# Two graph-attention blocks on one core: edge rows transposed on TensorE, wide one-hots, four reordered steps, and a weight chunk's low part moved to GpSimd

## The reference

```python
def gat_conv(x, src, dst, W, a_src, a_dst, b, heads, out_ch):
    h = (x @ W).reshape(n, heads, out_ch)
    alpha_src = jnp.einsum('nhc,hc->nh', h, a_src)
    alpha_dst = jnp.einsum('nhc,hc->nh', h, a_dst)
    e = jax.nn.leaky_relu(alpha_src[src] + alpha_dst[dst], 0.2)
    p = jnp.exp(e - segment_max(e, dst)[dst])
    alpha = p / segment_sum(p, dst)[dst]
    return segment_sum(h[src] * alpha[:, :, None], dst).reshape(n, heads * out_ch) + b
# block 0, self loops added to src and dst:
h = jax.nn.elu(gat_conv(x, src, dst, W1, a_src1, a_dst1, b1, 8, 768))
out = gat_conv(h, src, dst, W2, a_src2, a_dst2, b2, 1, 768)
```

## Time and profile before

| | |
|---|---|
| median of 3 runs | 361.6 us (361.49 to 362.41) |
| the profiled execution's own time | 363.34 us |
| span of its profile | 361.5 us |
| mean granted TensorE clock | 0.993 |
| TensorE (PE) busy | 349.8 us, 97% |
| VectorE (DVE) busy | 213.7 us, 59% |
| ScalarE (ACT) busy | 218.7 us, 60% |
| GpSimd (POOL) busy | 242.5 us, 67% |

### The profile page before, as it was taken

How to read it: one execution, slowest core, us unless ns; L and a number is a source line. 1 busy time by engine, 2 the same in 40 slices (tenths; PEclk the granted TensorE clock), 3 DMA queues, 4 the chain that set the end, 5 groups by cost and what they waited for, 6 DMA issues and landing times.

```text
span 361.5 us, 6079 instructions
## 1 busy us (share of the span) xinstructions
PE 349.8 (97%) x2058; PEld 300.3 (83%) x2060; DVE 213.7 (59%) x545; ACT 218.7 (60%) x376; POOL 242.5 (67%) x163
## 2 busy tenths in 40 slices
PE   7999999899999999999999999999999999999994
PEld 3888888788988988998898898888767888788883
DVE  4999872436418235553641834455687797953776
ACT  5897595637754864673775486467276867264601
POOL 2389659483883967669397496856256898687911
PEclk9999999899999999999999999999999999999999
DMA  7888967356556546574654665567162657337002
GB/s 248 284 301 227 397 229 258 130 176 173 175 163 198 166 170 188 169 244 130 222 178 136 214 172 174 188 167 245 57 199 94 181 190 196 131 113 233 5 2 87
DMA packets 24544, 65.15 MB, mean 180 GB/s; under 512 B 1952, under 2 KB 3024, under 8 KB 24528
## 3 DMA queue, kind: packets, MB, share of 16 engines
q1 hardware_dynamic: 20864, 55.02, 45.7%
q10 hardware_dynamic: 3664, 9.92, 10.0%
HBM read 64.15 MB, written 0.79 MB: 180 GB/s over the span
## 4 chain that ended last, share of the span: by engine, by line
PE 79%; DMA 4%; DVE 4%; POOL 4%; issue 4%; ACT 3%; DVEq 0%; POOLq 0%; SPq 0%
PE ps L1006 56%; PE ps L1296 9%; PE ps L1094 6%; POOL ring_lo L370 3%; DMA raw<-in_L_gnn_W 3%; PE ps L1128 2%; PE ps L1360 2%; DMA b_rows<-in_L_gnn_b 1%; PE ps L1073 1%; ACT ring_hi L357 1%; PE ps L1058 1%; DVE stats L1740 1%; DVE ps L1960 1%; POOL x_sb L634 1%; DVE z L1967 1%
## 5 line engine op out<-in xcount | busy, mean ns | idle before, releaser
L370 POOL TENSOR_TENSOR ring_lo<-raw,ring_hi 128x768 fp32r<-128x768 f32 x92 | 167.1, 1850 | 75.6 <-ACT ring_hi L357 75.6
L357 ACT ACTIVATE ring_hi<-raw 128x768 fp32r<-128x768 f32 x96 | 77.4, 839 | 40.0 <-PE ps L1006 28.9
L386 POOL TENSOR_TENSOR ring_lo<-raw,ring_hi 128x512 fp32r<-128x512 f32 (+1 forms) x40 | 59.4, 1512 | 20.3 <-ACT ring_hi L379 20.2
L1006 PE MATMUL ps<-ring_hi,zT_hi 128*128 128x256 f32 (+1 forms) x256 | 69.3, 346 | 0.9 <-ACT zT_hi L808 0.9
L1006 PE MATMUL ps<-ring_lo,zT_hi 128*128 128x256 f32 (+1 forms) x256 | 67.1, 337 | 0.0
L1006 PE MATMUL ps<-ring_hi,zT_lo 128*128 128x256 f32 (+1 forms) x256 | 66.8, 338 | 0.0
L1513 DVE CUSTOM_DVE_ANT_0 e<-ps,att 128x768 f32<-128x768 f32 x38 | 34.2, 953 | 49.0 <-PE ps L1006 49.0
L1006 PE MATMUL ps<-ring_hi,xT_hi 128*128 128x512 f32 x192 | 52.0, 347 | 2.1 <-DVE zT_lo L1662 1.8
L1006 PE MATMUL ps<-ring_hi,xT_lo 128*128 128x512 f32 x192 | 50.5, 341 | 0.0
L1006 PE MATMUL ps<-ring_lo,xT_hi 128*128 128x512 f32 x192 | 50.5, 339 | 0.0
L1006 PEld LDWEIGHTS ps<-ring_hi,zT_hi 128*128 128x128 f32 x256 | 42.0, 189 | 7.1 <-ACT zT_hi L808 1.6
(11 more groups left out here) (172 smaller groups left out, 545.1 us busy)
## 6 DMA issues: line engine op xcount, KB each, us to landing
raw<-in_L_gnn_W SPq DMA_DIRECT2D x54, 768.0 KB, 4.4
raw<-in_L_gnn_Wr SPq DMA_DIRECT2D x8, 768.0 KB, 4.5
att<-in_L_gnn_a_src ACTq DMA_DIRECT2D x10, 384.0 KB, 3.7
att<-in_L_gnn_a_dst ACTq DMA_DIRECT2D x10, 384.0 KB, 4.9
raw<-in_L_gnn_W SPq DMA_DIRECT2D x4, 384.0 KB, 5.1
x_sb<-in_x SPq DMA_DIRECT2D x3, 256.0 KB, 4.9
rows_hc<-in_L_gnn_b SPq DMA_DIRECT2D x1, 512.0 KB, 7.8
rows_hc<-in_L_gnn_g SPq DMA_DIRECT2D x1, 512.0 KB, 8.6
```

What stands on the lines that cost most here:

```text
L357: eng.activation(slot_hi(c), raw_chunk(c), ACT.Copy).then_inc(hi_done, 1)
L370: eng.tensor_tensor(slot_lo(c), raw_chunk(c), slot_hi(c).bitcast(F32), ALU.subtract)\
L386: eng.tensor_tensor(ring_lo[:, q["ring_at"]:q["ring_at"] + w], raw[:, q["raw_group"], q["raw_at"]:q["raw_at"] + w], ring_hi[:, q["ring_at" ...
L1006: last = pe.matmul(ps[:, at + to:at + to + hi - lo], a, b[:, lo:hi], start=start and n == 0 and to != D, stop=stop and n == PASSES - 1, sk ...
```

## The change

Seven edits, all in block 0's first two heads and the opening:

1. Head 1 on ScalarE: the DMAs of head 2's attention rows go behind the six splits of phase 3, just ahead of `elu(1)`. In the loop the order stays as it was.
2. Head 0 on VectorE: the fourth attention dot of head 1 goes from ahead of `elu(0)` to behind its first piece.
3. Edge lists: loaded as 64 rows of 128 edges, cast, transposed on TensorE in chunk 0, copied from PSUM. The edges of a tile are thus other ones; their sum is the same.
4. Input: x's first two chunks get separate high parts; chunks 0 and 2 begin with the pass that needs only high parts; the third part of x uses the first one's place in PSUM, behind a wait. The warm-up is cut, the bias rows' DMA goes ahead of the first split and their transpose from chunk 1 to chunk 2.
5. Steps 20 to 31 carry the weight (two per-partition scalars each; steps 26 to 31 count from below with negative weight).
6. One-hots 20 to 31 are made without a weight, by two wide operations.
7. FIRST = 3: GpSimd makes chunk 3's low part, and the second load of phase 1 waits for it.

The diff, cut to its core (declarations of tiles and semaphores are left out):

```diff
DVE_CH = CH - POOL_CH
-FIRST = 4
+FIRST = 3
 PHASES = 2 * H0
...
 AM_AT = [T_AT, S_AT + N]
-XT_AT = 0
+XT_AT = [0, BANK, 2 * BANK, 2 * BANK + N, 0, N]
 B1_AT = T_AT
+EDGES_AT = S_AT + N + 2 * ET
 STEPS_AT = T_AT + N - 1
...
 STEPS_EARLY = 5
+BELOW_FROM = (ACT_STEPS + ET) // 2
+PLAIN = ((ACT_STEPS, 24), (24, ET))
 PACK = 4096.0
...
-            if isinstance(p, int) and p == 1 and 2 * (g + 1) <= FIRST:
-                sp.wait_ge(lo_by["dve"], 2 * (g + 1))
-            else:
+            if isinstance(p, int) and p == 1 and 2 * g < FIRST:
+                sp.wait_ge(lo_by["dve"], min(2 * (g + 1), FIRST))
+            if not (isinstance(p, int) and p == 1 and 2 * (g + 1) <= FIRST):
                 sp.wait_ge(lo_by["pool"], POOL_CH * p - POOL_CH + 2 * (g + 1) - FIRST)
...
     load_x(0)
-    sp.dma_start(edges[:, 0, :], src.rearrange("(p t) -> p t", p=P)).then_inc(edges_loaded, 16)
-    sp.dma_start(edges[:, 1, :], dst.rearrange("(p t) -> p t", p=P)).then_inc(edges_loaded, 16)
+    sp.dma_start(edge_rows[0:ET, :], src.rearrange("(t p) -> t p", p=P)).then_inc(edges_loaded, 16)
+    sp.dma_start(edge_rows[ET:2 * ET, :], dst.rearrange("(t p) -> t p", p=P)).then_inc(edges_loaded, 16)
     sp.dma_start(raw[:, 0, D:2 * D], w1[:, 1, 0, :]).then_inc(raw_full[0], 16)
...
     pool.wait_ge(b2_loaded, 16)
-    pool.wait_ge(xT_ps, 3)
+    pool.wait_ge(xT_ps, 4)
     for i in range(NT):
...
     act.activation(rstd[:, 0:1], half[:, :], ACT.Exp)
+    act.dma_start(b1_rows[:, :], b0_b1.rearrange("(t p) -> t p", p=P)).then_inc(b1_loaded, 16)
...
-    def input_hi(b):
-        act.wait_ge(xT_ps, b + 1)
-        act.activation(xT_hi[:, 2 * b:2 * b + 2, :].rearrange("p k n -> p (k n)"),
-                       ps[:, XT_AT + b * BANK:XT_AT + (b + 1) * BANK], ACT.Copy).then_inc(xT_hi_done, 1)
+    def input_hi(first, chunks, at_done):
+        act.wait_ge(xT_ps, at_done)
+        act.activation(xT_hi[:, first:first + chunks, :].rearrange("p k n -> p (k n)"),
+                       ps[:, XT_AT[first]:XT_AT[first] + chunks * N], ACT.Copy).then_inc(xT_hi_done, 1)
     split_hi(act, FIRST_PHASE, 0, reused=False)
-    act.dma_start(b1_rows[:, :], b0_b1.rearrange("(t p) -> t p", p=P)).then_inc(b1_loaded, 16)
-    input_hi(0)
+    input_hi(0, 1, 1)
+    input_hi(1, 1, 2)
     split_hi(act, FIRST_PHASE, 1, reused=False)
...
     split_hi(act, FIRST_PHASE, 2, reused=False)
-    input_hi(1)
+    input_hi(2, 2, 3)
     steps(3, 5)
     split_hi(act, FIRST_PHASE, 3, reused=False)
-    input_hi(2)
+    input_hi(4, 2, 4)
     load_att(0, b0_as1[0:1, :], b0_ad1[0:1, :], D, reused=False)
...
         exps(h, (1, 0))
-        after_exps(h, last)
-    def after_exps(h, last=False):
         att_for(h + 1, last)
+        after_exps(h)
+        elu(h)
+    def after_exps(h):
         for c in range(4):
...
             split_hi(act, 2 * h + 1, c)
-        elu(h)
...
     after_exps(1)
+    att_for(2)
+    elu(1)
     with act.Fori(2, H0 - 1) as h:
...
-    def keep_warm(times, at):
+    def keep_warm(times, at, width=BANK):
...
         for _ in range(times):
-            pe.matmul(ps[:, at:at + BANK], zeros[:, 0:P], zeros[:, :], start=True, stop=True)
+            pe.matmul(ps[:, at:at + width], zeros[:, 0:P], zeros[:, 0:width], start=True, stop=True)
...
     pe.wait_ge(zeros_set, 1)
-    keep_warm(8, PROJ)
+    keep_warm(7, PROJ)
+    keep_warm(2, PROJ, P)
...
         pe.wait_ge(x_loaded[b], 16)
+        if b == 2:
+            pe.wait_ge(xT_lo_done, 1)
         for k in (2 * b, 2 * b + 1):
             for i in range(NT):
-                at = XT_AT + k * N + i * P
+                at = XT_AT[k] + i * P
                 last = pe.transpose(ps[:, at:at + P], x_sb[:, i, k * P:(k + 1) * P], ident[:, :])
-        last.then_inc(xT_ps, 1)
+            if b == 0 or k % 2 == 1:
+                last.then_inc(xT_ps, 1)
     transpose_x(0)
-    keep_warm(2, PROJ + 2 * BANK)
     for c in range(CH):
-        if c == 1:
+        if c == 2:
             pe.wait_ge(b1_loaded, 16)
...
         if c in (0, 2):
-            pe.wait_ge(xT_hi_done, c // 2 + 1)
-            chunk(FIRST_PHASE, c)
-            for passes in (FIRST_TWO, LAST_ONE):
+            pe.wait_ge(xT_hi_done, c + 1)
+            pe.wait_ge(hi_done, c + 1)
+            for passes in ((0,), (1,), LAST_ONE):
+                if passes == (1,):
+                    chunk(FIRST_PHASE, c)
                 if passes is LAST_ONE:
                     pe.wait_ge(xT_lo_done, c // 2 + 1)
+                if passes is LAST_ONE and c == 0:
+                    pe.wait_ge(edges_cast, 1)
+                    pe.wait_ge(iota_cast, 2)
+                    pe.transpose(ps[:, EDGES_AT:EDGES_AT + 2 * ET], edge_rows_f[:, :],
+                                 ident[0:2 * ET, 0:2 * ET]).then_inc(edges_ps, 1)
                 for i in range(NT):
...
         for t in range(ET):
-            pe.wait_ge(hot_done, t + 1)
+            pe.wait_ge(hot_done, t + 1 if t < ACT_STEPS else ACT_STEPS + sum(first <= t for first, _ in PLAIN))
             if t < ACT_STEPS:
...
     def input_lo(b):
-        dve.wait_ge(xT_hi_done, b + 1)
-        dve.tensor_tensor(xT_lo[:, 2 * b:2 * b + 2, :].rearrange("p k n -> p (k n)"),
-                          ps[:, XT_AT + b * BANK:XT_AT + (b + 1) * BANK],
-                          xT_hi[:, 2 * b:2 * b + 2, :].rearrange("p k n -> p (k n)").bitcast(F32),
+        dve.wait_ge(xT_hi_done, b + 2)
+        at, apart = XT_AT[2 * b], XT_AT[2 * b + 1] - XT_AT[2 * b]
+        of = ps[:, at:at + 2 * apart].rearrange("p (k n) -> p k n", k=2)[:, :, 0:N]
+        dve.tensor_tensor(xT_lo[:, 2 * b:2 * b + 2, :], of, xT_hi[:, 2 * b:2 * b + 2, :].bitcast(F32),
                           ALU.subtract).then_inc(xT_lo_done, 1)
...
     dve.tensor_copy(iota_ps, iota_i).then_inc(iota_cast, 1)
+    def plain_hots(first, end):
+        at = (first % per_home) * 2 * N
+        home = hot_homes[first // per_home][:, at:at + (end - first) * 2 * N]
+        shape = [P, end - first, P]
+        dve.tensor_tensor(home.rearrange("p (t n) -> p t n", n=2 * N)[:, :, 0:P],
+                          iota_ps[:, 1:1 + P].rearrange("p (t n) -> p t n", t=1).to_broadcast(shape),
+                          row_of[:, first:end].rearrange("p (t n) -> p t n", n=1).to_broadcast(shape),
+                          ALU.is_equal).then_inc(hot_done, 1)
...
     split_lo(dve, FIRST_PHASE, 0)
+    dve.wait_ge(edges_loaded, 32)
+    dve.tensor_copy(edge_rows_f[:, :], edge_rows[:, :]).then_inc(edges_cast, 1)
     input_lo(0)
-    dve.wait_ge(edges_loaded, 32)
-    dve.tensor_copy(edges_f[:, :, :], edges[:, :, :]).then_inc(edges_cast, 1)
-    dve.wait_ge(edges_cast, 1)
+    dve.wait_ge(edges_ps, 1)
+    dve.tensor_copy(edges_f[:, :, :].rearrange("p s t -> p (s t)"), ps[:, EDGES_AT:EDGES_AT + 2 * ET])\
+       .then_inc(edges_placed, 1)
+    dve.wait_ge(edges_placed, 1)
     dve.tensor_scalar(src_bias[:, :], edges_f[:, 0, :], -1.0, 0.5, ALU.mult, ALU.add).then_inc(src_biased, 1)
...
     dve.tensor_tensor(row_of[:, :], edges_f[:, 1, :], upper[:, :], ALU.subtract).then_inc(edges_split, 1)
-    for at, end, scale in ((0, ACT_STEPS, 1.0), (ACT_STEPS, ET, 2.0)):
+    for at, end, scale in ((0, ACT_STEPS, 1.0), (ACT_STEPS, BELOW_FROM, 2.0), (BELOW_FROM, ET, -2.0)):
         dve.tensor_scalar(weight_of[:, at:end], upper[:, at:end], scale * (PACK + 1.0) / P, -scale,
...
         for t in range(first, end):
-            dve.tensor_scalar(step(t), iota[:, :], edges_f[:, 0, t:t + 1], -0.5, ALU.is_ge, ALU.add)\
-               .then_inc(step_dve_done, 1)
+            dve.tensor_scalar(step(t), iota[:, :], edges_f[:, 0, t:t + 1], weight_of[:, t:t + 1],
+                              ALU.is_lt if t >= BELOW_FROM else ALU.is_ge, ALU.mult).then_inc(step_dve_done, 1)
...
     dve.wait_ge(iota_cast, 2)
+    dve.wait_ge(edges_split, 5)
     late_steps(ACT_STEPS, ACT_STEPS + STEPS_EARLY)
...
     late_steps(ACT_STEPS + STEPS_EARLY, ET)
-    split_lo(dve, FIRST_PHASE, 3)
     input_lo(2)
...
        .then_inc(b1_ready, 1)
-    dve.wait_ge(edges_split, 4)
-    hots(0, ET)
+    hots(0, ACT_STEPS)
+    for first, end in PLAIN:
+        plain_hots(first, end)
...
-    def elu(h):
+    def elu(h, between=None):
         for q in range(3):
+            if q == 1 and between is not None:
+                between()
             if q >= 1:
...
     dots(1, a_s, 0, a_src_done)
-    dots(1, a_d, 1, a_dst_done)
-    elu(0)
+    dots(1, a_d, 1, a_dst_done, tiles=(0,))
+    elu(0, between=lambda: dots(1, a_d, 1, a_dst_done, tiles=(1,)))
     dve.wait_ge(z_lo_done, 3)
...
```

More of the change, by code:

```diff
@@ L139, in build_gnn @@
         iota = sb("iota", [P, 1 + N], BF16)
-        edges = sb("edges", [P, 2, ET], I32)
+        edge_rows = sb("edge_rows", [2 * ET, P], I32)
+        edge_rows_f = sb("edge_rows_f", [2 * ET, P])
         edges_f = sb("edges_f", [P, 2, ET])
@@ L244, in build_gnn @@
         edges_cast = sem("edges_cast")
+        edges_ps = sem("edges_ps")
+        edges_placed = sem("edges_placed")
```

## The result

The changed kernel takes 365.63 us (median of 6 runs, 364.8 to 367.84), the kernel before on the same chip 361.55 (6 runs, 361.37 to 363.55): ratio 1.0099, 95% interval 1.0072 to 1.0126. It is slower by 4.1 us by the medians and by 3.6 by the ratio, where 3.5 less had been forecast. Rival (b), the alternating hold, had given 365.7. The six times fall into two groups, 364.8 to 364.9 and 366.3 to 367.8; the profiled execution is of the lower one.

What follows compares the result with a forecast made beforehand. The prediction took TensorE, busy 97% of the span, as the bound; 3.6 + 0.65 + 0.6 - 1.4 = 3.5 us off the median 361.6 gave 358.1 us, range 356.0 to 361.8.

Steps and rivals of the forecast that it cites:

- Rival (b): Opening: GpSimd's low parts and VectorE's late steps alternate; 7.2 stall and 1.8 clock on 356.7 give 365.7; chance 0.22.
- Part (5): Opening, chunk 3's low part on GpSimd: one hold against VectorE's seven late steps, costing 1.4; bounds 0 and 7.2.
- Part (1): Passage to head 2: moving its attention-row DMAs makes head 2 a steady head, 3.6 off; bounds 0 and 3.64.
- Part (2): Head 0's elu: with the fourth dot behind its first piece, VectorE and TensorE start earlier, 0.65 off.
- Part (3): Opening: chunk 1 starts at 9.45, chunk 2 at 12.2 against 12.72; with chunk 4's wait, 0.6 off.
- Part (4): Steps and one-hots: seven late steps 1.9, two wide one-hots 1.9, sums wait for TensorE's edge count, not them; 0.
- the 0.16 that chunk 4 was said to wait: Opening: chunk 4's wait for GpSimd at 17.05 before the change, counted towards the opening's 0.6.

Runs made afterwards that it cites:

- experiment 1: The changed kernel with chunk 3's low part back on VectorE, all else kept: 360.01 us, ratio to the kernel before 0.9962.
- experiment 7: The changed kernel with chunk 3's low part back on VectorE and the full warm-up of before restored: 359.88 us, ratio to the kernel before 0.9945.
- Experiment 6: The kernel before, unchanged, run once more for its trace: 361.37 us.
- experiment 4: The kernel before with only chunk 3's low part moved to GpSimd, steps keeping one per-partition scalar: 362.04 us, ratio 1.0003.
- experiment 5: The kernel before with only the two reorderings of heads 0 and 1, run twice: 359.26 us and 359.1 us.
- experiment 9: The kernel before with the two reorderings and the bias rows' DMA early, their transpose at chunk 2, run twice: 359.11 us and 358.81 us.
- experiment 8: The kernel before with the two reorderings and the changed kernel's short warm-up: 359.95 us, ratio 0.9938.
- experiment 3: The changed kernel with the last part of xT_lo made ahead of the seven late steps: 365.32 us, ratio to the kernel before 1.012.
- experiment 2: The changed kernel with the seven late steps reading iota from PSUM instead of SBUF: 360.85 us, ratio to the kernel before 0.9959.

## Why the prediction was wrong

**Part (5), the low part on GpSimd, is the step that failed.** It charged "one hold", 1.4, out of bounds of 0 and 7.2. The mechanism was named rightly, one engine holds the other, and its size chosen wrongly: the hold is paid anew for every step that meets GpSimd at work. "Two steps may follow each other so closely that nothing gets between" was the argument against rival (b); the timeline shows that each GpSimd operation does get between. The part cost 5.0 (experiment 1). The rows give the same: chunk 4 starts at 21.27, and with the low part on VectorE at 17.87 (experiment 7's profile). That is 3.4, and the low clock adds 1.7. The 3.4 are less than the stall of 3.93 because in experiment 7's profile x's transposes begin 0.26 later (5.56 against 5.30) and TensorE waits 0.18 for chunk 3's low part.

Rival (b) named the right mechanism, with 7.2 of stall and 1.8 of clock. Its stall was too long: it took five holds and the steps between them on top, where there were four, and it had TensorE ask for chunk 4 at 16.4 instead of 17.3. That its sum, 365.7, met the result is luck: it charged 9.0 for a hold of 5.6 (3.93 and 1.7), and it started from 356.7, where the kernel without GpSimd's part takes 360.0 (experiment 1). The 3.4 too much and the 3.3 too little cancel; the 3.3 are the next points.

**Part (1), head 2, was right in the profile and worth less in the runs.** Head 2 became a steady head as forecast. But the forecast took 3.6 from an execution of 363.3 us and subtracted it from a median of 361.6. Experiment 6 shows 1.6 in an execution of 361.4: pause 1.36, no low clock; experiment 4's profile shows 1.8. So 3.6 was some 2.0 too much. The price of the low clock belonged to that execution; why it fell there and not in the two others stays open.

**Part (2), head 0's elu, was right:** TensorE's first z product starts at 42.85 in experiment 5's profile, 43.57 before: 0.7 against 0.65.

**Part (3), the opening, was wrong:** 0.6 forecast, about -0.2 at chunk 2 (12.88 against 12.72). x landed at 5.16 instead of 4.8 (experiment 9, which only moves the bias rows, shows a delay of that size), and the edges' way over TensorE put VectorE's chain back: src_bias at 8.34, the low part of chunk 1 at 8.98 to 9.93, for which TensorE waited 0.60. The wait for the bias rows was removed, and one for VectorE took its place; experiment 9, which keeps the edges' old way, starts chunk 1 at 9.23. The cut warm-up was priced at nothing. It costs some 0.85 alone (experiment 8, on one chip), and the upper groups of the kernels that have it together with the halved input stand some 1.5 above their lower ones; that the warm-up makes these groups is likely from experiment 7 and not shown. With part (5) and the warm-up undone, the opening, steps and one-hots together still stand 0.6 to 0.8 us behind the reorderings alone (experiment 7's 359.88 against 359.1 to 359.26; the intervals of the ratios overlap). A small term was misread as well: the 0.16 that chunk 4 was said to wait isn't in the rows, which mark no wait there (14.91 and 2.1 give 17.0, and it started at 17.05).

**Part (4), steps and one-hots:** the free prices were right (seven steps 1.89 for 1.9, two wide one-hots 1.80 for 1.9), and so was 0 where VectorE was free: in experiment 7's profile TensorE waits for no step and no one-hot. Its cover failed: with the steps held, the one-hots lasted to 29.5 instead of 25.3, and experiment 3 shows what that costs once chunk 4 doesn't hide it, 5.1 us.

**The sum.** 3.5 faster was forecast and 4.1 slower measured, 7.6 apart. Part (5) is 3.6 of it (5.0 for 1.4), part (1) some 2.0, and the opening some 1.3 (0.6 forecast, 0.6 to 0.8 lost). The rest of 0.7 is about what the median stands above the lower group of the changed kernel's times.

## What to carry to other kernels

Before work is moved to GpSimd, look at what VectorE does in the same microseconds: each short SBUF-to-SBUF scalar operation there can cost a whole GpSimd operation, so many short ones are the worst company. An operand in PSUM avoided it here (experiment 2), and a lead of a microsecond over GpSimd left one step held instead of four (experiment 4). Price a hold by the number of operations that meet it. And take a stall's price only from an execution as fast as the median that it is subtracted from.

## What the runs showed that was not expected

In these traces the hold falls nearly all on VectorE: a step takes 1.85 to 1.91 where seven free ones take 1.89, and GpSimd's four operations 7.28 where they took 7.26. GpSimd isn't quite untouched. Its operation that starts while a step is running takes 1.97 instead of 1.84:

```profile
15.02 1.97 POOL L378 TENSOR_TENSOR ring_lo<-raw,ring_hi 128x768 fp32r<-128x768 f32 x1 [0.34 <-ACT ring_hi L365]
```

Experiment 4 has 1.92 in the same place. Whether a long VectorE operation would hold GpSimd for its whole length was not tried.

TensorE ran near half pace between 5.4 and 9.5 us in experiment 1's profile with a granted clock of 1.00 in every window, so in the opening a matmul's own duration says more than that column. The idle time ahead of x's transposes does not decide it alone: they took 0.63 behind 0.60 (the change) and behind 0.95 (experiment 3), but 1.09 behind 0.75 (experiment 1) and 1.02 behind 0.37 (experiment 8).
